# Weighing the keys of half the heads with high and low halves in a gated cross-attention and expert kernel

## The reference, cut to what matters

```python
# x (32, 128, 128), ctx (32, 128, 64); 16 heads of 64; batch size of the loop is one b
x = x + tanh(g_xattn) * xattn(layernorm(x), ctx)      # q @ Wq, ctx @ Wk, ctx @ Wv, softmax, @ Wo + bo
x = x + tanh(g_ffn)   * ffn(layernorm(x))             # 32 experts, 8 picked, and one shared MLP
# in xattn, for each batch and head:
scores = einsum('bhnd,bhmd->bhnm', q, k) / 8
attn   = softmax(scores)
out    = einsum('bhnm,bhmd->bhnd', attn, v)           # then @ Wo
```

## Time and profile before

| what | before |
|---|---|
| median of the runs | 667.65 us |
| the profiled execution | 665.77 us, its span 664.0 us |
| TensorE busy | 650.2 us, 98% |
| VectorE busy | 499.3 us, 75% |
| ScalarE busy | 365.4 us, 55% |
| GpSimd busy | 284.2 us, 43% |
| granted TensorE clock | 1.00 over the whole span |

### The profile page before, as it was taken

How to read it: one execution, slowest core, us unless ns; L and a number is a source line. 1 busy time by engine, 2 the same in 40 slices (tenths; PEclk the granted TensorE clock), 3 DMA queues, 4 the chain that set the end, 5 groups by cost and what they waited for, 6 DMA issues and landing times.

```text
span 664.0 us, 13629 instructions
## 1 busy us (share of the span) xinstructions
PE 650.2 (98%) x3668; PEld 472.1 (71%) x3668; DVE 499.3 (75%) x1331; ACT 365.4 (55%) x690; POOL 284.2 (43%) x316
## 2 busy tenths in 40 slices
PE   8999999999999999999999999999999999999997
PEld 5656666666667676676658778788887878888785
DVE  6989857777586775867787979968696877869565
ACT  3564556565465654655556455565655555555553
POOL 4222323233131332324202656656565656656553
PEclk9999999999999999999999999999999999999999
DMA  7323323232322323223225735273644536364650
GB/s 186 98 64 82 92 65 79 62 84 63 83 75 68 90 63 80 64 78 94 52 67 138 174 89 131 74 182 85 156 119 111 130 72 156 85 159 112 133 141 16
DMA packets 63276, 65.58 MB, mean 99 GB/s; under 512 B 26112, under 2 KB 41600, under 8 KB 63232
## 3 DMA queue, kind: packets, MB, share of 16 engines
q1 hardware_dynamic: 63232, 65.07, 39.9%
HBM read 61.64 MB, written 2.88 MB: 97 GB/s over the span
## 4 chain that ended last, share of the span: by engine, by line
PE 68%; issue 8%; POOL 8%; DVE 6%; DMA 5%; SPq 3%; ACT 1%; POOLq 0%; DVEq 0%; ACTq 0%
PE bank L1151 12%; PE bank L1227 12%; PE bank L1152 11%; PE bank L1153 11%; POOL halves L516 7%; PE bank L1251 6%; PE bank L1187 4%; PE bank L1207 2%; PE bank L1216 2%; PE bank L1210 2%; PE bank L1213 2%; DVE area L806 2%; DMA inverse_dram<-inverse 1%; DMA inverse_bc<-inverse_dram 1%; SPq L294 1%
## 5 line engine op out<-in xcount | busy, mean ns | idle before, releaser
L516 POOL TENSOR_TENSOR halves<-area,halves 128x512 fp32r<-128x512 f32 x134 | 174.0, 1299 | 141.0 <-ACT halves L650 136.5
L663 ACT ACTIVATE area<-bank 128x512 f32<-128x512 f32 x136 | 81.4, 598 | 109.3 <-PE bank L1153 106.7
L602 ACT ACTIVATE area<-bank 128x512 f32<-128x512 f32 x128 | 69.5, 595 | 117.3 <-PE bank L1216 117.3
L1107 DVE TENSOR_TENSOR bank<-area,bank 128x512 f32<-128x512 f32 x128 | 88.6, 692 | 51.1 <-PE bank L1153 50.8
L1227 PE MATMUL bank<-area,ctx_keys 128*65 128x512 f32 (+1 forms) x256 | 124.6, 599 | 0.2 <-ACT u_odd L550 0.2
L1151 PE MATMUL bank<-x2t_hi,w_hi 128*128 128x512 f32 x272 | 110.3, 405 | 1.4 <-DVE area L1118 1.3
L1152 PE MATMUL bank<-x2t_hi,w_lo 128*128 128x512 f32 x272 | 107.1, 394 | 0.0
L1153 PE MATMUL bank<-x2t_lo,w_hi 128*128 128x512 f32 x272 | 106.3, 391 | 0.0
L462 POOL TENSOR_TENSOR ctx_hi<-ctx_raw,ones_col 128x128 fp32r<-128x128 f32 x32 | 18.8, 588 | 197.3 <-DMA ctx_raw<-ctx_t 197.3
L792 DVE TENSOR_REDUCE row_max<-bank 128x4 f32<-128x512 f32 x128 | 81.7, 680 | 25.4 <-PE bank L1187 21.0
L650 ACT ACTIVATE halves<-area 128x512 fp32r<-128x512 f32 x136 | 85.1, 626 | 21.1 <-DVE area L1118 20.7
(11 more groups left out here) (129 smaller groups left out, 1087.7 us busy)
## 6 DMA issues: line engine op xcount, KB each, us to landing
wbc<-rows_dram SPq DMA_DIRECT2D x126, 256.0 KB, 4.4
inverse_bc<-inverse_dram SPq DMA_DIRECT2D x64, 256.0 KB, 3.9
w_raw<-experts SPq DMA_DIRECT2D x32, 102.0 KB, 2.0
ctx_raw<-ctx_t SPq DMA_DIRECT2D x32, 64.0 KB, 1.9
ctx_keys<-ctx_nat SPq DMA_DIRECT2D x32, 64.0 KB, 2.1
out<-area SPq DMA_DIRECT2D x7, 256.0 KB, 4.1
max_rows<-max_t SPq DMA_DIRECT2D x64, 4.0 KB
area<-wq_t SPq DMA_DIRECT2D x1, 512.0 KB, 4.4
```

What stands on the lines that cost most here:

```text
L516: nc.gpsimd.tensor_tensor(hid_lo[:, u % SLOTS, :], hid[:, u % HIDS, :], raw(hid_hi[:, u % SLOTS, :]), ALU.subtract).then_inc(hidlo_ready, 1)
L602: nc.scalar.activation(probs_t[:, k, :, :], st_ps[q][:].rearrange("p (h n) -> p h n", h=4), ACT.Exp)\
L663: nc.scalar.activation(silu_g[:, u % 2, :], gate_ps[u % 2][:], ACT.Silu).then_inc(silu_ready, 1)
L1107: nc.vector.tensor_tensor(up_ps[u % UPS][:], silu_g[:, u % 2, :], up_ps[u % UPS][:], ALU.mult)\
```

## The change

In chunks 1 to 6 the weighing of h=0 is done in three fp32r matmuls for each q (`weigh_halves`) in place of one fp32 product. h=1 and chunks 0 and 7 stay as they were. The halves of the keys are made by GpSimd (`split_keys`, two instructions of 128 x 192 in each batch, ahead of the expert weights), the high half of the probabilities by ScalarE (`probs_high`, two copies of 128 x 512 in each batch: after `max_out` in odd batches, after the two `u_out` of t-1 in even ones), the low half by VectorE (`probs_low`, two subtractions of 128 x 512). The halves lie in buffers that are free in the attention. VectorE's order in the loop is a function of its own, `steady_attention`: `probs_low` comes after `batch_stats` (in even batches after `normalise(t-2, 0)`); in odd batches `normalise(t-2, 0)` moves behind the second pair of `take_max` and `invert`; in b=0 `ln_apply` comes ahead of `residual`. `normalise` waits for the DMA of its own q only, by one semaphore for each q.

```diff
@@ buffers
+        p_hi = [x[:, 1, :] for x in (x2t_hi, x2t_lo)]
+        p_lo = [x[:, 0, :] for x in (x2t_hi, x2t_lo)]
+        tail = slice(WCOLS - 2 * 3 * CD, WCOLS)
+        keys_hi, keys_lo = (w[:, tail].rearrange("p (s n) -> p s n", s=2) for w in (w_hi, w_lo))
@@ GpSimd
+            def split_keys(b, t, c):
+                pool.wait_ge(keys_in[b], 16 * c + 16)
+                wait(pool, u_done, 4 * (t - 2) + 4)
+                nc.gpsimd.tensor_tensor(keys_hi[:, b % 2, :], ctx_keys[:, b, :], ones_col[:].broadcast_to([P, 3 * CD]),
+                                        ALU.mult).then_inc(keyshi_ready, 1)
+                pool.wait_ge(keyshi_ready, t + 1 - HALVED_FROM)
+                nc.gpsimd.tensor_tensor(keys_lo[:, b % 2, :], ctx_keys[:, b, :], raw(keys_hi[:, b % 2, :]), ALU.subtract)\
+                    .then_inc(keyslo_ready, 1)
@@ ScalarE
+            def probs_high(t):
+                act.wait_ge(exp_ready, 4 * t + 2)
+                wait(act, u_done, 4 * t - 2)
+                for q in range(2):
+                    nc.scalar.activation(p_hi[q], probs_t[:, q, :, :].rearrange("p h n -> p (h n)"), ACT.Copy)\
+                        .then_inc(phi_ready, 1)
...
+                    if not first and not last and b % 2 == 1:
+                        probs_high(t)
                     if not (first and b == 0):
                         for q in range(2):
                             u_out(t - 1, (b - 1) % 2, 1, q)
+                    if not first and not last and b % 2 == 0:
+                        probs_high(t)
@@ VectorE
+            def probs_low(t):
+                for q in range(2):
+                    dve.wait_ge(phi_ready, 2 * (t - HALVED_FROM) + q + 1)
+                    wait(dve, u_done, 4 * (t - 1) + q + 1)
+                    nc.vector.tensor_tensor(p_lo[q], probs_t[:, q, :, :].rearrange("p h n -> p (h n)"),
+                                            raw(p_hi[q]), ALU.subtract).then_inc(plo_ready, 1)
...
-                dve.wait_ge(inverse_in, 32 * t + 32)
+                dve.wait_ge(inverse_in[q], 16 * t + 16)
...
+            def steady_attention(c):
+                for b in range(CB):
+                    t = CB * c + b
+                    for q in range(2):
+                        take_max(t + 2, b % 2, 0, q)
+                    batch_stats(t - CB, b)
+                    if b % 2 == 0:
+                        normalise(t - 2, b % 2, 0)
+                    probs_low(t)
+                    if b == 1:
+                        xt_low(c + 1)
+                    for q in range(2):
+                        take_max(t + 2, b % 2, 1, q)
+                    invert(t - 1, (b - 1) % 2)
+                    if b % 2 == 1:
+                        normalise(t - 2, b % 2, 0)
+                    normalise(t - 2, b % 2, 1)
+                    if b == 0:
+                        ln_apply(c + 1, t - b + CB)
+                    if b % 2 == 1:
+                        g_low(2 * c + 2 + b // 2, b // 2)
+                    residual(t - 3)
+                    batch_mean(t - CB, b)
+                    if b == CB - 1:
+                        keep_means(t - b - CB)
@@ TensorE
+            def weigh_halves(t, b, q):
+                if q == 0:
+                    pe.wait_ge(keyslo_ready, t + 1 - HALVED_FROM)
+                pe.wait_ge(phi_ready, 2 * (t - HALVED_FROM) + q + 1)
+                wait(pe, u_ready, 4 * (t - 1) + q + 3)
+                cols = slice(0, CD + 1) if q == 0 else slice(CD, 3 * CD)
+                ps = u_ps[q][0:CD + 1 if q == 0 else P, :]
+                nc.tensor.matmul(ps, keys_hi[:, b % 2, cols], p_hi[q], start=True, stop=False)
+                nc.tensor.matmul(ps, keys_lo[:, b % 2, cols], p_hi[q], start=False, stop=False)
+                pe.wait_ge(plo_ready, 2 * (t - HALVED_FROM) + q + 1)
+                nc.tensor.matmul(ps, keys_hi[:, b % 2, cols], p_lo[q], start=False, stop=True).then_inc(u_done, 1)
```

More of the change, by code:

```diff
@@ L70 @@
 STATS_AT = {2: (2,), 3: (3,), 4: (4,), 5: (5,), 6: (6, 7)}
+HALVED_FROM = CB
 NB_SEAM = (NCH - 2) * CB
@@ L316, in spread_inverse @@
                     sp.dma_start(inverse_bc[rows(q), :, :].rearrange("p h n -> p (h n)"),
-                                 inverse_dram[parity, q:q + 1, :].broadcast_to([HD, 2 * CT])).then_inc(inverse_in, 16)
+                                 inverse_dram[parity, q:q + 1, :].broadcast_to([HD, 2 * CT])).then_inc(inverse_in[q], 16)
             def load_diag(diag, w, q, arrived):
@@ L499, in attention @@
                     t = CB * c + b
+                    if not first and not last:
+                        split_keys(b, t, c)
                     split_weights(b % 2, t, 2 * c + b // 2, NB if last else t + CB)
@@ L1019, in attention @@
                                 chunk_stats(n)
-                        if h == 1 and b % 2 == 1 and not last:
+                        if h == 1 and b % 2 == 1 and first:
                             g_low(2 * c + 2 + b // 2, b // 2)
@@ L1031, in attention @@
                                 rstd_level(0, 1, slice(CB, 2 * CB), level)
-                        elif not last and step_of_chunk == 1:
-                            ln_apply(c + 1, t - b + CB)
                         if last:
@@ L1044, in attention @@
                             normalise(t - 2, b % 2, 0)
-                        if step_of_chunk == 2 and not last:
-                            xt_low(c + 1)
+                        if step_of_chunk == 2 and first:
+                            xt_low(1)
                         if step_of_chunk == 3 and last:
@@ L1051, in attention @@
                                 rstd_level(0, 2, slice(2 * CB, NB), level)
-            in_chunks(dve, attention)
+            def steady_attention(c):
[23 more added lines that the diff above has]
+                        keep_means(t - b - CB)
+            attention(0, True, False)
+            with dve.Fori(1, NCH - 1) as c:
+                steady_attention(c)
+            attention(NCH - 1, False, True)
             residual(NB - 3)
@@ L1321, in attention @@
                     scores(t, b, 2 * c + b // 2, 1, 2 * c + b // 2 + 1, None)
-                    weigh(t, b, 0, 0, c + 1)
+                    if first or last:
+                        weigh(t, b, 0, 0, c + 1)
+                    else:
+                        weigh_halves(t, b, 0)
                     if last and b == 0:
@@ L1326, in attention @@
                         g_project(b // 2, c + 1, ((max_ready, 4 * (t + 2) + 3), (exp_ready, 4 * t + 3)))
-                    weigh(t, b, 0, 1, c + 1)
+                    if first or last:
+                        weigh(t, b, 0, 1, c + 1)
+                    else:
+                        weigh_halves(t, b, 1)
             pe.wait_ge(neg_ready, 2)
```

5 lines of the change are left out of this document (4 added, 1 removed).

## The result

The changed kernel took 677.31 us (median of five runs, 674.99 to 677.73) against 667.65 us before: 9.7 us more. The ratio of the runs is 1.0135, 95% interval 1.0122 to 1.0149. It was measured once more on another chip: 1.0119 (1.0099 to 1.0139). The forecast was 676.2 us, slower.

A forecast was written before the change was run, and what follows sets the result against it. TensorE was taken to set the pace, with thin leads of the other engines where the change adds work. +0.65 + 0.20 - 0.41 + 0.98 = +1.42 us a chunk, +8.5 in six, gave 667.65 + 8.5 = 676.2 us, range 663 to 681.

The forecast's parts named there:

- M: Reference point in each batch: the start on TensorE of the second maximum scores (h=1).
- The residual behind `ln_apply`: b=0 into b=1: four ln_apply delay the residual, so TensorE's transposition of the maxima stalls 1.06 us; +0.65 a chunk.
- The moved `normalise`: Odd batches: normalise(q=0) behind invert delays u_out, g_high and the next scores; 0.98 us later in b=3, 0.2 in b=1.
- The copies push the sums: b=3: two ScalarE copies, 1.23 us, stand ahead of the last u_out; sums land at M + 2.43, invert goes at M + 2.5.
- The saving: TensorE's weighing of h=0: six fp32r matmuls at 1.46 us replace 1.87, 0.41 saved a batch; bounds 0.25 and 0.49.
- No wait for the low halves: b=0: second low half ready at about M + 0.85, TensorE needs it at M + 1.6, so no wait.
- The split wait gives nothing here: normalise waiting only for its own q's inverse: no gain, since even normalise(q=0) has 1 us or more in hand.
- The sum of a steady chunk: Loop chunk: +0.65 (b=0 into b=1), +0.20 (rest of b=1), -0.41 (b=2), +0.98 (b=3), together +1.42 us.
- D: Rival: VectorE and GpSimd hold each other up, some 1 us a chunk more, 682 us; chance 0.12.
- C: Rival: only the residual is hidden, its bank free earlier than read; +0.36 us a chunk, 669.8 us; chance 0.08.
- Rival A: TensorE stays the bound everywhere; 1.74 us saved a chunk, 10.4 us in all, 657.2 us; chance 0.10.
- B: Rival: only the moved normalise is hidden, the residual holds; -0.68 us a chunk, 663.6 us; chance 0.09.

The follow-up runs named there:

- the order alone: Changed kernel with weighing as before in all batches and no halves, keeping VectorE's new order and the split wait: 670.89 us beside 665.04 before, ratio 1.0086.
- the old order: Changed kernel with residual ahead of ln_apply, odd batches' normalise(q=0) ahead of the second take_max; halves and split wait kept: 657.81 us beside 665.04, again 658.61 beside 667.46.
- the split wait alone: Kernel before with one semaphore for each q on the inverse's DMA, nothing else changed: 662.88 us beside 667.27, ratio 0.9937.
- the residual first: Changed kernel with residual and batch_mean ahead of ln_apply again in b=0: 668.37 us beside 665.04 before, ratio 1.0047.

## Why the prediction was right

Point by point, from the chunk of the time lines above (M as in the prediction, us):

| step | before | predicted | measured |
|---|---|---|---|
| b=0: end of the residual | M + 3.89 | M + 5.55 | 120.03 - 114.33 = M + 5.70 |
| transposition of b=1 | M + 5.00 | M + 5.65 | 120.13 - 114.33 = M + 5.80 |
| its wait | 0 | 1.06 | 1.05 |
| b=1: `u_out`, then the next scores | scores at M + 7.58 | M + 3.8, M + 7.8 | M + 3.31, M + 7.13 |
| b=2, scores to scores | 8.75 | 0.41 less | 8.45, 0.30 less |
| b=3: `invert` | M + 3.0 | M + 2.5 | 147.11 - 144.76 = M + 2.35 |
| b=3: `u_out` | M + 2.72 | M + 4.06 | M + 3.84 |
| b=3: next scores | M + 7.14 | M + 8.13 | M + 7.75 |
| steady chunk | 41.86 | +1.42 | +1.16 |

- *The residual behind `ln_apply`*: right in place and size, and shown by undoing it, 1.16 us a chunk. A term in it was undersized: the four `ln_apply` take 1.98 us and not 1.58. They began 0.2 sooner than the sum had them (M + 3.52), so the residual ended just 0.15 later. One term was missing: behind the wait TensorE also takes 0.14 us longer to M of b=1 (4.28 us from the transposition, before 117.39 - 113.25 = 4.14).
- *The moved `normalise`*: right in place. The stated chain (ScalarE's `u_out`, `g_high` at 2.65 us, 0.87 to the scores) was mis-sized. `g_high` takes 2.04 to 2.14 when it starts late. In the kernel before the four copies of b=3 started 0.63 to 0.71 us apart (142.12, 142.75, 143.46, 144.17), in step with `g_project`, whose banks follow each other by 0.71; here they start 0.48 apart (149.10 and, two later, 150.05). VectorE's own line, which I had just inside of it, is the bound (`g_low` ends at 152.37, the scores start at 152.51). So b=3 lost 0.61 and not 0.98, and b=1 gained 0.45 where I had 0.20 lost. But that gain is one against the longer chunk of the rows alone: in steady chunks the kernel before takes 7.12 to 7.21 us there, the changed one 7.12.
- *The copies push the sums*: shown, `invert` waited 0.36 us, did not wait in the run of the order alone, which has no copies, and 0.45 a chunk came back when `normalise` did not wait with it.
- *The saving*: two weighings take 117.44 - 115.90 = 1.54 us, not 1.46, against 1.87: 0.33 a batch, not 0.41. As predicted, only b=2 keeps it.
- *No wait for the low halves*: right. The six matmuls come 0.23 to 0.24 apart, 0.29 behind the first, and the next product starts 0.32 behind the last; these two steps are what 1.46 had too little of.
- *The split wait gives nothing here*: in VectorE's new order this was not tested. In the old one it was wrong by far, 0.48 us a chunk in the kernel before and 1.89 with the halves. I had seen two DMAs issued 0.5 us apart and no more.
- *The sum of a steady chunk*: predicted +0.65 + 0.20 - 0.41 + 0.98 = +1.42. Steady chunk against steady chunk it is +0.79 and +0.15 (the wait for the residual and what follows it), about 0 for b=1, -0.32 for b=2 and +0.64 for b=3: +1.2, as the transpositions say (+1.16). The wait for the residual was dearer than predicted, b=3 cheaper.
- *The total*: 8.5 us predicted. The two executions of the changed kernel whose clock stayed at 1.000 took 673.8 and 673.9 beside 667.46, so at full clock the change costs 6.4 us. What is left of the 9.7, some 3 us, is the clock in chunks 1 and 2, which no step of the prediction had. That 676.2 came so near to 677.3 is luck in part: the chunks were put 2 us too high, and the clock was left out.
- *Slips in the working*: forecast, D and most of C add up to about 0.79, not 0.75, and 0.5 in both b=1 and b=3 of six chunks is 6.0, not 5.5. Neither moves the forecast.

Rival A (657.2, 10.4 us less, TensorE the bound everywhere) is not reached even in the old order: that gives 7.2 and 8.9 us less on two chips, of which a steady chunk's 0.48 is the split wait. Its condition was the right one to watch, and the change itself broke it: the moved `normalise` would have had to end before M + 2.7, the residual before M + 4.5, and it ended at M + 5.70. B fell with the wait for `g_low`, C with the 1.05 us wait. D had its signs, but small: `ln_apply` was stretched (below), about 0.4 us on a held path once a chunk, not 1.

A chunk in parts, by the runs: split wait -0.48, three fp32r matmuls -0.92, making the halves 0, together 40.47. The new order +2.55: 1.16 for `ln_apply` ahead of the residual, 0.45 for the `normalise` behind the wait for the sums, 0.7 for `normalise` behind `take_max` (41.20 against 40.47), and 0.2 that only the two together show. Without the halves the same order costs 42.80 - 41.38 = 1.42, so more than half of its loss is there without the added work.

## What to carry to other kernels

When work is added to an engine that is not the bound, look for the place where that engine already stood idle for a DMA and put it there, and leave all else in its order: in this kernel 5.5 us of added work a chunk cost nothing there, and an order that looked better on paper cost 2.5, 1.4 of it without the added work. A busy share near 100% does not show that the engine is the limit: in this kernel a wait of VectorE's, split in two, took 0.5 us off such a chunk. For each instruction that is moved, write down what it releases and the time at which the bound engine asks for it, in the first batch after it too (here a residual whose only reader was a transposition one batch later). Two transfers that fill halves of one buffer for two instructions deserve a semaphore each.

## What the runs showed of the hardware

The four `ln_apply` (one SBUF input each, two scalars from SBUF) took 1.58 us before, 1.62 in the run of the new order alone, and 1.98 in the changed kernel, whose order is the same but whose GpSimd also makes the halves of the keys. Behind the residual they took 1.58 with the split wait alone and 2.17 with the halves of the keys. GpSimd was at work beside them, first on the context, then on the keys; its time line from the changed kernel, with VectorE's `normalise` at 116.59 and `ln_apply` at 117.85:

```profile
116.93 1.15 POOL L471 TENSOR_TENSOR ctx_hi<-ctx_raw,ones_col 128x128 fp32r<-128x128 f32 x1 [8.53 <-DMA ctx_raw<-ctx_t]
118.16 0.46 POOL L474 TENSOR_TENSOR ctx_lo<-ctx_raw,ctx_hi 128x128 fp32r<-128x128 f32 x1
118.57 0.51 POOL L481 TENSOR_TENSOR w_hi<-ctx_keys,ones_col 128x192 fp32r<-128x192 f32 x1
```

The same instruction on the context took 0.40 us in the kernel before (at 141.50), and 1.15 here, beside a VectorE product of two SBUF tensors: it ended at 118.08, 0.27 us after that product (117.81). The Trainium skill's page "SBUF — State Buffer" (section "Who interferes with whom") says that a VectorE instruction with two SBUF inputs contends with a GpSimd one that reads SBUF, and that `tensor_scalar`, which `ln_apply` is, can contend with GpSimd as well. The 1.15 us agree with the first; the 1.98 against 1.62 agree with the second, though no run shows in which mode `ln_apply` ran. Held back the most was GpSimd, which had time.

And the kernel with the residual first, whose steady chunk is that of before (41.86 us), ran 3.3 us slower (668.37 beside 665.04). Its three executions at clock 0.999 or 1.000 took 665.8, 666.3 and 667.3 us, so about 2 of these 3.3 are the clock. In the traces idle times of 1 to 2 us on TensorE were followed by some us at half clock, though not each time, and with products that compute nothing put in the idle times of the changed kernel the clock stayed at 0.999 or 1.000 in all four executions.
